# A three-layer graph network on one core: ten dense tiles instead of eight in the first layer, its count pieces built earlier, and other tails

## The reference

```python
deg = segment_sum(ones, dst); dinv = rsqrt(deg)          # loops included
def conv(h, W, b):
    xw = h @ W
    return segment_sum(xw[src] * (dinv[src] * dinv[dst])[:, None], dst) + b
h = conv(conv(conv(x, W1, b1), W2, b2), W3, b3)
out = layernorm(x + h)                                   # over the 512 features, eps 1e-5
```

## Time and profile before

| | |
|---|---|
| median of three runs | 2267.77 us (2265.42 to 2273.44) |
| the profiled execution: its time / its span | 2270.13 us / 2268.3 us |
| busy: PE, DVE, ACT, POOL | 88%, 65%, 35%, 71% |
| mean granted TensorE clock | 0.946 |
| gathers, their busy time | 1632, 1571.8 us |
| chain that ended last, by engine | POOL 30%, PE 24%, issue 10% |
| layer 0, first gather to layer 1's first | 119.0 to 1007.5 us |
| layer 1, the same to layer 2's first | 1007.5 to 1631.4 us |
| layer 2, to the end of the span | 1631.4 to 2268.3 us |

### The profile page before, as it was taken

The page is one execution under the profiler, slowest core; times in us unless marked ns, Lnnn a source line. Parts: engine busy times, 40 slices in busy tenths (PEclk is TensorE's granted clock), DMA queues, the critical chain, the costliest instruction groups (busy, mean ns, idle before and its releaser), DMA issues.

```text
span 2268.3 us, 32947 instructions
## 1 busy us (share of the span) xinstructions
PE 2003.9 (88%) x10202; PEld 1146.9 (51%) x10202; DVE 1483.9 (65%) x3679; ACT 798.3 (35%) x1502; POOL 1600.7 (71%) x1680
## 2 busy tenths in 40 slices
PE   6664778998989987769999999999799999999986
PEld 6321224444444532225666666666366666666653
DVE  8635775777777764435555555556677777777777
ACT  0502553444444433223333333333333333333321
POOL 0177777777777777737777777777577777777774
PEclk7777898999999999889999999999899999999998
DMA  8666887888888888848888888888788888899986
GB/s 291 227 198 196 265 278 224 247 253 242 242 279 277 278 259 244 250 143 245 249 245 251 250 257 269 279 280 274 249 258 265 270 271 268 286 306 300 287 271 222
DMA packets 286715, 580.98 MB, mean 256 GB/s; under 512 B 72916, under 2 KB 132241, under 8 KB 286545
## 3 DMA queue, kind: packets, MB, share of 16 engines
q0 software_dynamic: 131344, 429.32, 62.0%
q1 hardware_dynamic: 155200, 149.59, 20.0%
HBM read 511.68 MB, written 67.06 MB: 255 GB/s over the span
## 4 chain that ended last, share of the span: by engine, by line
POOL 30%; PE 24%; issue 10%; DMA 2%; DVE 1%; ACT 0%; DVEq 0%; POOLq 0%; ACTq 0%
POOL ring L1017 30%; PE ps L1353 16%; PE ps L1240 5%; DMA ring<-y_dram,kept 2%; PE ps L1251 1%; PE ps L1282 1%; PE ps L1252 0%; DVE acc L2199 0%; PE ps L1336 0%; DVE acc L1987 0%; PE ps L1404 0%; DVE ln L2055 0%; DMA y_dram<-acc 0%; DVE dense_first L2168 0%; PE ps L1310 0%
## 5 line engine op out<-in xcount | busy, mean ns | idle before, releaser
L1017 POOL DMA_INDIRECT ring<-y_dram,kept x1632 | 1571.8, 963 | 547.0 <-issue 488.8
L1240 PE MATMUL ps<-ring,onehot 128*32 128x512 f32 x3264 | 463.3, 633 | 95.8 <-DMA ring<-y_dram,kept 94.9
L2199 DVE SCALAR_TENSOR_TENSOR acc<-ps,acc 128x512 f32<-128x512 f32 x494 | 341.0, 690 | 259.5 <-PE ps L1353 233.7
L1353 PE MATMUL ps<-dense_first,wide_a 128*128 128x512 f32 x1144 | 317.2, 399 | 13.2 <-ACT wide_a L1593 6.2
L1593 ACT CAST wide_a<-onehot 128x512 fp32r<-128x512 uint8 (+1 forms) x297 | 173.1, 594 | 284.6 <-PE ps L1353 185.5
L1353 PEld LDWEIGHTS ps<-dense_first,wide_a 128*128 128x128 f32 x1144 | 212.1, 190 | 101.1 <-ACT wide_a L1593 19.1
L1353 PE MATMUL ps<-dense_next,wide_a 128*128 128x512 f32 x820 | 237.2, 398 | 0.5 <-DVE acc L2199 0.5
L1952 DVE TENSOR_TENSOR onehot<-ps,kept 128x128 f32<-128x128 f32 x414 | 118.5, 287 | 162.5 <-PE ps L1240 161.2
L1353 PE MATMUL ps<-dense_first,y_rows 128*128 128x512 f32 x756 | 211.1, 401 | 2.1 <-DVE dense_next L2168 1.3
L1240 PEld LDWEIGHTS ps<-ring,onehot 128*32 128x32 f32 x3264 | 68.6, 109 | 257.2 <-issue 244.4
L1554 ACT CAST ring<-ps 128x490 uint8<-128x490 f32 x228 | 154.0, 692 | 125.9 <-PE ps L1310 124.8
(11 more groups left out here) (289 smaller groups left out, 2345.7 us busy)
## 6 DMA issues: line engine op xcount, KB each, us to landing
onehot<-a_dram SPq DMA_DIRECT2D x456, 64.0 KB
ring<-y_dram,kept POOLq DMA_INDIRECT x1632, 4.9
y_dram<-acc SPq DMA_DIRECT2D x99, 256.0 KB, 11.9
a_dram<-ring SPq DMA_DIRECT2D x19, 784.0 KB, 5.7
acc<-in_x_dram SPq DMA_DIRECT2D x1, 12288.0 KB
y_dram<-acc SPq DMA_DIRECT2D x12, 1024.0 KB, 7.5
out_dram<-acc SPq DMA_DIRECT2D x48, 256.0 KB
w_sb<-in_x_dram SPq DMA_DIRECT2D x24, 256.0 KB
```

Of the source, the lines that this page charges most:

```text
L1017: pool.indirect_dma_start(ring[:, s, :], None, y_dram[layer], bass.IndirectOffsetOnAxis(ap=rows, axis=0)).then_inc(done, 16)
L1240: mm = pe.matmul(ps[k * WIDE:(k + 1) * WIDE, g % BANKS, :], wide_hot[:, r, k, :], ring[:, RING_ORDER[r] * CPQ + k, :], start=opens, stop=c ...
L1353: mm = pe.matmul(ps[:, bank, :], wide_slots[n % WIDE_SLOTS][:, P * k:P * (k + 1)], y_parts[(TILES * (layer - 1) + tile) % YSLOTS][:, part, :],
L2199: dve.scalar_tensor_tensor(out=rows, in0=ps[:, UNIT_BANKS[n % len(UNIT_BANKS)], :], scalar=0.5, in1=rows, op0=ALU.mult, op1=ALU.add).then_ ...
```

## The change

In layer 0 ten tiles are dense instead of eight, and the sparse part begins at chunk 154 instead of 118: 628 chunks are gathered instead of 664. The windows of the ten tiles are built six a quad; the other 117 come only after the dense units. The four chunks of the last group are one quad in every layer, each in its own 32 partitions, and the group before is placed and added ahead of that quad's sum. In layer 0's last two quads the products of finished tiles come before the sum of the quad; tile 47 is turned in the last quad and multiplied in `last_tile`, half of it before the last group is placed and half after. Layer 1's units end five instead of six quads before its last.

```diff
-EARLY_DENSE = 8
+EARLY_DENSE = 10
...
     def quad_chunks(own, a):
-        return [c for c in range(group_chunk(own) + a, group_chunk(own + 1), CPW) if c < USED]
+        if own == GROUPS - 1:
+            return list(range(group_chunk(own), USED)) if a == 0 else []
+        return list(range(group_chunk(own) + a, group_chunk(own + 1), CPW))
...
-    WIN_PACE = 4
+    WIN_PACE = 6
     EARLY_WINDOWS = EARLY_DENSE * WPT
-    REST_AT = WIN_AT + EARLY_WINDOWS // WIN_PACE + 1
-    REST_QUADS = LAYER_QUADS[0] - REST_AT - 6
...
-    UNITS0_FROM = REST_AT + 5
-    UNITS0_TO = LAYER_QUADS[0] - 10 - 3 * EARLY_DENSE
+    UNITS0_FROM = WIN_AT + EARLY_WINDOWS // WIN_PACE + 6
+    UNITS0_TO = LAYER_QUADS[0] - 11 - 3 * EARLY_DENSE
+    REST_AT = UNITS0_TO + 1
+    REST_QUADS = LAYER_QUADS[0] - REST_AT - 6
...
-    UNITS_TO = [0, DENSE_QUADS - 6, DENSE_QUADS - LAST_WINDOW]
+    UNITS_TO = [0, DENSE_QUADS - 5, DENSE_QUADS - LAST_WINDOW]
...
-    LOOP_TILES = TILES - 1
+    LOOP_TILES = [TILES - 2, TILES - 1, TILES - 1]
...
-        return DENSE_BANKS[w % 2] if w < EARLY_WINDOWS else BUILD_BANK
+        return DENSE_BANKS[w % 2]
...
             def last_tile(layer):
                 t = TILES - 1
+                if layer == 0:
+                    store(layer, t - 1)
...
-                for k in range(len(chunks_of(n))):
+                for k, c in enumerate(chunks_of(n)):
                     if closes_layer(n):
                         pe.wait_ge(last_gathered[k], 16 * (layer + 1))
-                    mm = pe.matmul(ps[k * WIDE:(k + 1) * WIDE, g % BANKS, :], wide_hot[:, r, k, :], ring[:, RING_ORDER[r] * CPQ + k, :],
-                                   start=opens, stop=closes, tile_position=(0, k * WIDE), skip_group_check=True)
+                    window, turn = divmod(c - group_chunk(own_of(g)), CPW)
+                    at = window * WIDE
+                    mm = pe.matmul(ps[at:at + WIDE, g % BANKS, :], wide_hot[:, r, k, :], ring[:, RING_ORDER[r] * CPQ + k, :],
+                                   start=(turn == 0), stop=(turn == CPW - 1 or c + 1 == USED), tile_position=(0, at), skip_group_check=True)
...
                 pe.wait_ge(win_hot, w + 1)
-                if w > EARLY_WINDOWS:
-                    pe.wait_ge(win_kept, w)
-                elif w > 1:
+                if w > 1:
                     pe.wait_ge(win_kept, w - 1)
+                if w >= EARLY_WINDOWS:
+                    pe.wait_ge(dense0_added, UNITS0)
...
+                    last = q == DENSE_QUADS - 1
+                    if last:
+                        place_group(g - 1)
                     sum_quad(QUAD_AT[layer] + q)
-                    if a == 0 and q > 0:
+                    if a == 0 and q > 0 and not last:
                         place_group(g - 1)
...
+                    late = q >= LAYER_QUADS[0] - 2
+                    if late:
+                        for t in finished_at(0, q):
+                            multiply_tile(TURN_OF[0][t], TURN_BANK)
+                    if q == LAYER_QUADS[0] - 1:
+                        place_group(g - 1)
+                        turn_done_tile(TILES - 2)
+                        sum_quad(q)
+                        continue
                     sum_quad(q)
...
             def last_tile(layer):
-                place_group(GROUP_AT[layer + 1] - 1)
                 if layer > 0:
+                    place_group(GROUP_AT[layer + 1] - 1)
                     return
+                pe.wait_ge(turn_copied, TILES - 1)
+                multiply_part(TURN_BANK, turned_sb, range(0, FB // 2))
+                place_group(GROUP_AT[1] - 1)
+                multiply_part(TURN_BANK, turned_sb, range(FB // 2, FB))
...
+                    if q == LAYER_QUADS[0] - 1:
+                        keep_turned(TILES - 2)
                     if q + 1 == QUADS_TO[g]:
                         copy_slots(g)
...
+                    late, last = q >= LAYER_QUADS[0] - 2, q == LAYER_QUADS[0] - 1
+                    if late:
+                        for t in finished_at(0, q):
+                            bias_rows(0, t, h_sb, TURN_BANK, TURN_OF[0][t])
+                    if last:
+                        add_group(g - 1)
                     finish_quad(q)
```

More of the change, by code:

```diff
@@ L214, in finish_quads @@
         if layer > 0:
-            sparse = [(first_quad(layer, LAST_GROUP[t] + 1), 0, t) for t in range(DENSE, LOOP_TILES)]
+            sparse = [(first_quad(layer, LAST_GROUP[t] + 1), 0, t) for t in range(DENSE, LOOP_TILES[layer])]
             return sorted(sparse + [(UNIT_QUAD[layer][UNITS - DENSE + t] + 1, 1, t) for t in range(DENSE)])
-        ready = sorted([(first_quad(0, LAST_GROUP[t] + 1) + 2, 0, t) for t in range(EARLY_DENSE, LOOP_TILES)]
+        ready = sorted([(first_quad(0, LAST_GROUP[t] + 1) + 2, 0, t) for t in range(EARLY_DENSE, LOOP_TILES[0])]
                        + [(UNIT0_QUAD[UNITS0 - EARLY_DENSE + t] + 3, 1, t) for t in range(EARLY_DENSE)])
@@ L306, in gcn_three_layers_resnorm @@
     assert all(r * TILE_FACTOR >> TILE_SHIFT == r // PARTS_PER_TILE for r in range(WIN_PARTS)) and P * WIN_BLOCKS * TILE_FACTOR < 1 << 24
-    assert all(sorted(t for q, late, t in finish) == list(range(LOOP_TILES)) for finish in FINISH)
-    assert all(LAST_GROUP[t] + 1 < GROUPS for t in range(LOOP_TILES)) and window_quad(WINDOWS - 1) < LAYER_QUADS[0] - 1
+    assert all(sorted(t for q, late, t in finish) == list(range(LOOP_TILES[layer])) for layer, finish in enumerate(FINISH))
+    assert all(LAST_GROUP[t] + 1 < GROUPS for t in range(LOOP_TILES[LAYERS - 1])) and window_quad(WINDOWS - 1) < LAYER_QUADS[0] - 1
     assert all(q < LAYER_QUADS[layer] for layer in range(LAYERS) for q, late, t in FINISH[layer])
     assert all(abs(a[0] - b[0]) > 1 for a, b in zip(FINISH[0], FINISH[0][1:])) and len(pair_of(0)) == PAIR and Y0_SLOTS == 2 * PAIR
-    assert all(len(windows_at(q)) <= WIDE0_SLOTS for q in UNIT0_QUAD) and REST_AT + 2 < UNITS0_FROM and (TILES - 1) % PAIR == 0
+    assert all(len(windows_at(q)) <= WIDE0_SLOTS for q in UNIT0_QUAD) and REST_AT > LAST_UNIT0_QUAD + 1 and (TILES - 1) % PAIR == 0
     assert all(SPLIT0_QUAD[b] < UNIT0_QUAD[b * EARLY_DENSE] for b in range(PAIRS0))
@@ L1230, in sum_quad @@
                 layer = layer_of(g)
-                opens, closes = a == 0, n + 1 == QUADS_TO[g]
+                opens = a == 0
                 pe.wait_ge(hot_ready, n + 1)
@@ L1255, in turn_done_tile @@
             def turn_done_tile(t):
-                turn = TURN_OF[0][t]
+                turn = TURN_OF[0].get(t, t)
                 if t < EARLY_DENSE:
@@ L1382, in first_layer @@
                         turn_done_tile(t)
-                    for t in finished_at(0, q):
-                        multiply_tile(TURN_OF[0][t], TURN_BANK)
+                    if not late:
+                        for t in finished_at(0, q):
+                            multiply_tile(TURN_OF[0][t], TURN_BANK)
                     build(q)
@@ L1402, in last_tile @@
                 pe.wait_ge(turn_copied, TILES)
-                for k in range(FB):
-                    mm = pe.matmul(ps[:, LAST_PRODUCT_BANK, :], last_turned[:, k * P:(k + 1) * P], w123[:, k, :],
-                                   start=(k == 0), stop=(k == FB - 1))
-                mm.then_inc(tile_multiplied, 1)
+                multiply_part(LAST_PRODUCT_BANK, last_turned, range(FB))
             def any_tile_product(t):
@@ L1611, in dense_layer @@
                             root_turn(TURN_OF[layer][t])
+                    last = layer < LAYERS - 1 and q == DENSE_QUADS - 1
+                    if last:
+                        for t in finished_at(layer, q):
+                            scale_rows(layer, t, h_sb, TURN_OF[layer][t])
                     if QUAD_AT[layer] + q + 1 == QUADS_TO[g]:
@@ L1617, in dense_layer @@
                             root_turn(TURN_OF[layer][t])
-                    if layer < LAYERS - 1:
+                    if layer < LAYERS - 1 and not last:
                         for t in finished_at(layer, q):
@@ L1649, in last_tile @@
                     act.activation(last_turned, ps[:, LAST_TURN_BANK, :], ACT.Copy).then_inc(turn_copied, 1)
+                    scale_rows(layer, TILES - 2)
                 if layer < LAYERS - 1:
@@ L1951, in stage_places @@
                 c = chunks_of(n)[0]
+                by = 1 if own_of(QUAD[n][0]) == GROUPS - 1 else CPW
                 dve.tensor_tensor(wide_hot[:, n % RING_QUADS, :, :], iota_ps[:, 0:WIDE].unsqueeze(1).broadcast_to([P, CPQ, WIDE]),
[L1953 removed]
+                                  lo_f[:, c:c + by * (CPQ - 1) + 1:by].unsqueeze(2).broadcast_to([P, CPQ, WIDE]),
                                   ALU.is_equal).then_inc(hot_ready, 1)
@@ L2217, in dense_layer @@
                             units += 1
-                    finish_quad(n)
+                    last = q == DENSE_QUADS - 1
+                    if not last:
+                        finish_quad(n)
                     if a == 0 and q > 0:
```

(9 more changed lines are left out.)

11 lines of the change are left out of this document (9 added, 2 removed).

## The result

The changed kernel takes 2306.1 us (median of 6 runs, 2295.2 to 2311.5) against 2268.8 of the kernel before (2265.4 to 2273.4): a ratio of 1.0158, 95% interval 1.0141 to 1.0176. It is 1.6% slower, where 0.5% faster was forecast, and it lies above the range. The profiled execution took 2305.2, its span 2303.1.

What follows compares the result with a forecast made beforehand. GpSimd's row gathers (5.01 us a quad) bound the kernel before, TensorE (c) after. Layer 0's -7.5, then +0.5 - 1.0 - 4, gave -12 us: 2256 against 2267.8 (2258 for the profiled execution), range 2230 to 2292.

Steps and rivals of the forecast that it cites:

- (c): Layer 0, quads 38 to 115, 3.2 dense units a quad: TensorE binds, 5.8 us a quad, 452 us.
- rival 1: Count-matrix pieces come late in (c): 6.24 us a quad, total 2291; chance 0.27 together with (a) at its worst.
- waits for additions: In (c), TensorE's third unit waits 0.81 us for VectorE in each group-opening quad, plus 0.15 a quad.
- TensorE's own work: Low bound of (c), opening quads without their wait and no other wait: 5.40 us a quad, 421 us.
- rival 2: TensorE keeps up better, opening quads in (c) don't wait: 5.40 us a quad, total 2225; chance 0.14.
- (a): Layer 0, quads 11 to 32, six count windows a quad on VectorE: 133 us, bounds 124 and 143.
- The rule weighed there: Two-port VectorE operations block GpSimd's DMA descriptors, slowing gathers in (a): 137 us at worst against 133.
- (d): Layer 0, quads 116 to 150, the other windows, 3.4 a quad: under the gathers' pace, 168 us, at worst 178.
- (e): Layer 0, quad 151 to the sum of 155, light quads: 17 us, mostly a product and two transposes.
- (f): Layer 0's tail behind the sum of quad 155: 19.5 us, or 21.2 if the last product stays slow.
- Layers 1 and 2: Same gathers in the bodies: +0.5 and 0 us; shorter tails: -1.0 in layer 1, -4 in layer 2.
- rival 4: Tails don't shrink, copies are the chain: 8 us of (f) missing, 2264; chance 0.23 shared with the nothing-measurable rival.

Runs made afterwards that it cites:

- run with later stores: Changed kernel with finished tiles' stores one quad later in the count-matrix loading queue while units run: 2275.5 us, 1.0038 of the kernel before.
- repaired kernel: Changed kernel with stores one quad later and a third PSUM bank for layer 0's units: 2233.5 us, 0.9862 of the kernel before.
- 8-tile run: Changed kernel with 8 dense tiles again, its moved windows and new tails kept: 2280.8 us, 1.0064 of the kernel before.

## Why the prediction was wrong

*The step that failed* is (c): "ScalarE waited for them 19 times already, 35.5 us. Against: TensorE's own waits in front of units stand under VectorE", and so 5.8 us a quad with ScalarE's waits hidden. At 3.2 units a quad they aren't hidden: TensorE stood 21.9 us for the widening, 22 times. Measured 6.19, 482.5 us against 452, which is 30.5 of the 47 us by which the profiled execution (2305.2) missed the 2258. It is rival 1 at nearly its price (6.24, 487 us). The run with later stores shows the cause by taking it away: with nothing else changed stage (c) falls to 454.9 us, within 3 us of the forecast (partly by luck, since the forecast's own work of TensorE was 8 us too high, see below). That kernel still takes 2275.5 us, 0.4% more than before: the other stages' 17 us, below, were missed as well. The argument against the rival was the error. In the trace of before, from 390 to 820 us, TensorE's wait for the widening was

```profile
PE ps L1336 <- ACT wide L1584: 2.1, 3, 1.3
```

so the next unit was nearly always still in hand; the row showed how little of ScalarE's 35.5 us reached TensorE and not how near the rest was to it. Four slots held the units of 1.8 quads, now of 1.25, and a store holds the queue up for about a quad (132.4 us in 21 waits before, 6.3 each): I had both numbers and didn't compare them.

*The waits for additions,* counted at 0.81 us for each opening quad and 0.15 for every quad (33 us in all), were right in kind and nearly in size: 28.1 us, 1.08 for each of 26 opening quads.

*TensorE's own work* was estimated at 5.40 us a quad as the low bound. With next to no waits it takes 5.30, 8 us less in the stage. So the bound, priced in rival 2, was nearly right, and the repaired kernel goes below it; the change as made couldn't.

*(a)* 135.0 us against 133; 6.14 a quad. VectorE is busy for 90%, and the clock didn't fall (0.94, before 0.92). Its wait for products was smaller than I had it (2.1 us, not 12.6), and it waits 8.2 us for windows instead. GpSimd waits 11.0 us for sums, and the ring hides what else is late. *The rule weighed there:* a gather takes 967 ns with six windows a quad, against 956 with four. 101 gathers by 11 ns are 1.1 us. One blocked operation of 0.30 us ahead of each gather, as the rule at its worst, would have made it 30. So the rule (the Trainium skill, SBUF — State Buffer, "SBUF: two separate sides") isn't borne out here at that size. Whether these operations hold both ports no trace shows. The stage's 135 us are VectorE's 121.5 of work and its waits.

*(d)* 171.2 against 168, and *(e)* 17.6 against 17: right. The 8-tile run shows what was near: with 5.1 windows a quad instead of 3.4 the same stage is over the gathers' pace.

*(f)* 23.3 against 19.5. The row of steps came as written, but its first one, the last sum (quad 156), was taken at 1.00 us and took 4.30:

```profile
1018.22 1.00 PE ps L1250 x8
1019.22 1.48 issue
...
1023.16 0.70 PE ps L1276 x4
1023.86 4.30 PE ps L1250 x8
1028.16 1.91 PE ps L1418 x4
...
1033.89 3.71 PE ps L1418 x8
```

That is the chain that ended last. Two things make the 4.30. The first is the clock. In the repaired kernel the same sum took 2.69 us at a granted clock of 1.00; here the clock was 0.62 over it, most of it at the lower level, 1.2 GHz, and 2.69 / 0.62 is 4.3. The stretch ahead of the sum and the sum itself here, then its line in the repaired kernel's chain, and the stretch around that:

```profile
1018.00:1023.90 5.90, 2.66 (x16) 0.99 (x16) 3.40 (x6) 1.21 (x3) 0.00 (x0) 0.98 0.12 44
1023.90:1028.00 4.10, 4.10 (x8) 0.72 (x8) 0.00 (x0) 0.59 (x1) 0.00 (x0) 0.62 0.00 0
...
956.56 2.69 PE ps L1255 x8
...
956.00:960.00 4.00, 4.00 (x14) 1.41 (x15) 0.38 (x2) 1.18 (x2) 0.00 (x0) 1.00 0.00 0
```

TensorE had been busy for 2.66 of the 5.9 us ahead of the sum, at a clock of 0.98.

The second is in the code, and the section on the change has it wrong, and so has the prediction, which let the merged quad put "four chunks into four column groups". The chunks of the last group do not have 32 partitions each. `sum_quad` takes the partitions from `divmod(c - group_chunk(own_of(g)), CPW)` with CPW = 3, and an ordinary quad has every third chunk of its group, so four different sets of 32 partitions; the last group's four chunks stand next to each other, so three of them go to set 0 and one to set 1 (the trace's placing of that group has `64x512`, two sets, where a full group has 128 partitions). An ordinary sum of eight matmuls, spread over four sets, takes 1.00 us; this one, with six of the eight in one set, 2.69 at the same clock. In the repaired kernel the sum's weight loads begin 0.43 us apart, and six matmuls in a row at that pace are 2.6 us, all eight would be 3.4 (estimates). The sum also waits for each chunk by itself, but with the data landed (DMA share 0.00) that costs nothing that the trace shows. It is so in every layer: in layers 1 and 2 of the changed kernel the last sum is

```profile
1654.42 4.79 PE L1250 MATMUL ps<-ring,onehot 128*32 128x512 f32 x8
...
2288.83 5.02 PE L1250 MATMUL ps<-ring,onehot 128*32 128x512 f32 x8
```

at clocks of 0.56 and 0.53, which is again 2.7 us each at full clock. Before, the same four chunks took three sums of 1.05, 1.04 and 1.04 us in layer 0, at a clock of 1.00. So the merge itself saved some 0.4 us of TensorE's time and not the 2 that "1.00 us like any other" counts on. That the shared set is the reason is read from the code and these rows; no run put the four chunks into four sets.

*Layers 1 and 2.* +2.2 and +1.9 us in the bodies against +0.5 and 0, -0.6 and -2.6 in the tails against -1.0 and -4: 5 us worse together. The signs of the tails are right and the gains smaller than thought. The last sums of 4.79 and 5.02 us, taken at 1.00, are a cause that the trace shows; rival 4's, the copies, wasn't needed.

*The range* ended at 2292, at rival 1's price with everything else as forecast. The stages beside (c), (f) and the later layers with 17 us together, put it over. I had given rival 1 and (a) at its worst 0.27, where the trace of before already had a queue that stood 132.4 us in front of stores.

## What to carry to other kernels

A wait that is hidden says nothing of how near it is to showing. When a change raises the rate of a stage, divide each prefetch's depth by the new rate and compare it with the longest time that the issuing queue can be blocked by something else; here that was four slots against stores that wait for a product. Two hand-overs in one loop can cover for each other: one repair gave 31 us, the other 12, both 73, so a repair that shows little alone should be tried with the other before it is dropped. And where matmuls are put into one quad so that they run side by side, look up in the code which partitions each of them writes.

## What the runs showed of the hardware that was not expected

Chips differ. On the second one the gathers of the kernel before (with later stores) take 1.48 us each in layer 1, 717.4 us for 484, where the first takes 1.255; on the third, in the repaired kernel, 1.49. The instructions themselves aren't longer; their queue waits:

```profile
L1023 POOL DMA_INDIRECT ring<-y_dram,kept x484 | 462.1, 955 | 286.3 <-issue 131.6 <-remote 86.4 <-PE ps L1246 37.3
```

955 ns each, with 286.3 us of idle time in front (30.9 of it before the layer's first gather), 86.4 of it booked as "remote", a releaser that no gather on the first chip has. What it is the trace doesn't show. The granted clock was lower there too, 0.94 in this layer against 0.99.

By the rows of the last sum, matmuls that write the same 32 partitions don't run side by side here: a sum of eight took 1.00 us spread over four sets of partitions and 2.69 with six in one set, both at a clock of 1.00.

And TensorE's busy time in this view isn't its work: the same matmuls (1896 and 1895 in the traces) filled 431.7 us over quads 38 to 115 with waits between them and 410.1 without, at a clock of 1.00 in both.
